# Merging the closing block of an attention and MLP kernel into the engines' main programs

## The reference

```
q = xn @ Wq (16 heads of 32); k, v = split(xn @ Wkv) (4 groups of 32)
scores = q k^T / sqrt(32), causal, + alibi slope * (s - t); attn = softmax(scores); o = attn @ v
attention = concat(o) @ Wo + bo
gate, up = xn @ Wg^T, xn @ Wu^T;  inter = gelu(gate) * up (4096 wide);  mlp = inter @ Wd^T
out = x + attention + mlp
```

## Time and profile before

| | |
|---|---|
| profiled execution | 1784.39 us, span 1782.6 |
| busy: PE, DVE, ACT, POOL | 95%, 75%, 60%, 53% of the span |
| PE's first matmul of the loop | at 120.18 |
| last matmul of the last slot | starts at 1688.39 |
| last sum of the MLP | DVE, starts at 1695.02, 0.69 us |
| granted clock, mean | 0.985 |

### The profile page before, as it was taken

The page is one execution under the profiler, slowest core; times in us unless marked ns, Lnnn a source line. Parts: engine busy times, 40 slices in busy tenths (PEclk is TensorE's granted clock), DMA queues, the critical chain, the costliest instruction groups (busy, mean ns, idle before and its releaser), DMA issues. The chain is left out here.

```text
span 1782.6 us, 31010 instructions
## 1 busy us (share of the span) xinstructions
PE 1693.1 (95%) x10368; PEld 848.4 (48%) x10368; DVE 1340.1 (75%) x2785; ACT 1075.6 (60%) x1779; POOL 953.2 (53%) x801
## 2 busy tenths in 40 slices
PE   4989999999999999999999999999999999999947
PEld 3754444444444444444444444444444444444435
DVE  6867777777777777777777777777777777777728
ACT  2436757575757676675757575766757575757610
POOL 3315647374646556473746465564737464645617
PEclk9989999999999999999999999999999999999968
DMA  6770120302020201203021202012030203020154
GB/s 190 208 195 16 29 59 17 75 24 74 26 72 20 75 17 44 56 16 80 20 73 26 74 20 74 16 47 52 20 80 17 73 26 74 23 70 17 48 176 149
DMA packets 94971, 110.04 MB, mean 62 GB/s; under 512 B 39085, under 2 KB 58541, under 8 KB 93021
## 3 DMA queue, kind: packets, MB, share of 16 engines
q1 hardware_dynamic: 94812, 108.05, 22.3%
HBM read 72.74 MB, written 22.41 MB: 53 GB/s over the span
## 5 line engine op out<-in xcount | busy, mean ns | idle before, releaser
L1409 POOL TENSOR_TENSOR plo<-p,phi 128x512 f16<-128x512 f32 (+1 forms) x576 | 659.0, 1151 | 327.8 <-ACT phi L1241 324.9
L1234 ACT ACTIVATE p<-score_ps,pshift 128x512 f32<-128x512 f32 (+1 forms) x576 | 382.1, 663 | 308.0 <-DVE score_ps L1321 154.4
L1241 ACT ACTIVATE phi<-p 128x512 f16<-128x512 f32 (+1 forms) x576 | 349.9, 607 | 15.3
L1417 POOL TENSOR_TENSOR il<-prod,ih 128x512 f16<-128x512 f32 x128 | 160.8, 1256 | 352.5 <-DVE ih L1315 352.5
L1141 PE MATMUL score_ps<-qst,kst 128*128 128x512 f32 (+3 forms) x640 | 308.0, 498 | 12.1 <-ACT p L1234 10.7
L1336 DVE TENSOR_REDUCE mxp<-max_ps 128x1 f32<-128x512 f32 x256 | 175.3, 685 | 53.9 <-PE max_ps L1119 53.9
L1283 DVE TENSOR_TENSOR acc<-down_ps,acc 128x512 f32<-128x512 f32 x253 | 172.7, 683 | 52.2 <-PE down_ps L1087 50.3
L1107 PE MATMUL gate_ps<-xh,wh 128*128 128x512 f16 x512 | 199.1, 389 | 0.0
L1107 PE MATMUL up_ps<-xh,wh 128*128 128x512 f16 x512 | 198.4, 387 | 0.0
L1087 PE MATMUL down_ps<-wh,ih 128*128 128x512 f16 x506 | 196.1, 387 | 0.9 <-DVE acc L1283 0.9
L1107 PE MATMUL gate_ps<-xh,wl 128*128 128x512 f16 x512 | 194.8, 380 | 0.0
(11 more groups left out here) (197 smaller groups left out, 2910.2 us busy)
## 6 DMA issues: line engine op xcount, KB each, us to landing
qst<-q_parts SPq DMA_DIRECT2D x204, 64.0 KB
kst<-k_parts SPq DMA_DIRECT2D x48, 256.0 KB, 4.7
o<-oraw SPq DMA_DIRECT2D x192, 64.0 KB
vst<-v_parts SPq DMA_DIRECT2D x17, 512.0 KB, 6.1
q_parts<-o SPq DMA_DIRECT2D x24, 256.0 KB, 3.4
raw<-L_ffn_gate_W_packed_dram SPq DMA_DIRECT2D x18, 256.0 KB, 2.8
raw<-n_L_ffn_up_W_packed_dram SPq DMA_DIRECT2D x18, 256.0 KB, 3.1
raw<-L_ffn_down_W_packed_dram SPq DMA_DIRECT2D x18, 256.0 KB, 3.9
```

The costliest lines, as they stand in the source:

```text
L1234: nc.scalar.activation(p32[n % PR][:, 0:cols], score_ps[:, 0:cols], ACT.Exp, bias=pshift[:, 0:1]).then_inc(exp_done, 1)
L1241: nc.scalar.activation(phi[n % PP][:, 0:cols], p32[n % PR][:, 0:cols], ACT.Copy).then_inc(phi_done, 1)
L1409: nc.gpsimd.tensor_tensor(plo[n % PP][:, 0:cols], p32[n % PR][:, 0:cols], phi[n % PP][:, 0:cols], ALU.subtract).then_inc(plo_done, 1)
L1417: nc.gpsimd.tensor_tensor(il[w % 2][:, a, :], prod[a][:], ih[w % 2][:, a, :], ALU.subtract).then_inc(il_done, 1)
```

## The change

The block `epilogue` is gone; what it did follows the loop in each engine's program, and parts of it stand in the last head.

- **Outputs as f16 pairs.** After `normalise` ACT rounds the head to f16 (`output_hi`, slot 38) and POOL takes the rest (`output_lo`, slot 39); `store_on` stores both, and the stored heads are loaded as operands without a conversion. `o_copy` no longer scales; the factor is applied at the very end (`yback`).
- **Wo as f16 pairs**, in the last head: SP loads it into the room of the decoded weights when the head starts; DVE finds its largest value (slots 26 to 29), a DRAM round trip spreads it (`spread_tops`), DVE makes the scale (slot 33), ACT and DVE the pair (slots 35 to 40). In that head nothing of a next head is loaded, decoded or turned.
- **Bias in the first sums.** The preamble stores the column scales and their inverses; the first sum into each tile of `acc` takes `bias * inverse` instead of cleared memory.
- **Row sums apart.** `gather_o` issues two transfers for them instead of four, ahead of the others, with a semaphore of their own.
- **Order after the loop.** PE projects two tiles before the MLP's last sums and six behind them, always the three full groups, in all eight banks; then the last group of these eight, and then the other eight tiles. ACT issues 18 transfers (x, stored heads) and then does the last `output_hi`; the results are made in `acc` and stored from it.

```diff
+    def output_hi(act, h):
+        act.wait_ge(on_done, h + 1)
+        if h:
+            act.wait_ge(on_out, 32 * h)
+        nc.scalar.activation(onh[:], on[:], ACT.Copy).then_inc(ohi_done, 1)
...
+    def output_lo(pool, h):
+        pool.wait_ge(ohi_done, h + 1)
+        if h:
+            pool.wait_ge(on_out, 32 * h)
+        nc.gpsimd.tensor_tensor(onl[:], on[:], onh[:], ALU.subtract).then_inc(olo_done, 1)
```

Preamble's SP, at its end, and the start of the loop:

```diff
                 store_v(NCH - 1)
+                sp.wait_ge(os_done, 1)
+                    sp.dma_start(os_s[0].rearrange("(k p) -> p k", p=P), oscale[:]).then_inc(os_out, 16)
+                    sp.dma_start(os_s[1].rearrange("(k p) -> p k", p=P), oinv).then_inc(os_out, 16)
...
+                sp.wait_ge(os_out, 32)
+                for row, src in ((column_inv, os_s[1]), (bias, bo)):
+                    sp.dma_start(row, src.rearrange("(o n) -> o n", o=1).broadcast_to([P, C])).then_inc(bias_in, 16)
...
-                nc.gpsimd.memset(acc[:], 0.0).then_inc(acc_done, 1)
+                pool.wait_ge(bias_in, 32)
+                nc.gpsimd.tensor_tensor(bias_row, bias, column_inv, ALU.mult).then_inc(acc_done, 1)
```

PE, ACT, DVE and SP after the loop:

```diff
+                pe.wait_ge(wo_lo, KVH)
+                pe.wait_ge(o_in[0], 16 * FULL_DMAS[0])
+                pe.wait_ge(red_done, after(HEADS * NMAX))
+                for n in range(2):
+                    project(n, first)
                 pe.wait_ge(gelu_done, after(HEADS * GU))
...
                 for t in range(TPC):
                     for half in range(2):
                         down(HEADS * NCH - 1, t, half, (down_ps, gate_ps, up_ps, score_ps)[t])
+                pe.wait_ge(oraw_done, after(2 * HEADS * NCH))
+                for n in range(2, TPC):
+                    project(n, first)
+                pe.wait_ge(o_in[1], 16 * FULL_DMAS[1])
+                for t in range(TPC):
+                    pe.wait_ge(acc_done, after((HEADS * NCH - 1) * TPC + t + 1))
+                    project(TPC + t, first)
+                for n in range(NT):
+                    if n % TPC == 0:
+                        pe.wait_ge(o_in[n // TPC], 16 * (FULL_DMAS[n // TPC] + 2))
+                        pe.wait_ge(last_in[n // TPC], 32)
+                    if n >= len(y_ps):
+                        pe.wait_ge(y_read, n - len(y_ps) + 1)
+                    project(n, last if n < len(y_ps) else range(KVH))
...
+                act.wait_ge(il_done, after(HEADS * GU))
+                load_x(act, 1)
+                act.wait_ge(on_out, 32 * LAST)
+                for c in range(2):
+                    load_rest(act, c)
+                act.wait_ge(up_done, HEADS * GU)
+                for c in range(2, NCH):
+                    load_x(act, c)
+                for c in range(2, NCH):
+                    load_full(act, c)
+                    load_rest(act, c)
+                output_hi(act, LAST)
+                act.wait_ge(ohi_done, HEADS)
+                load_last(act, 0, onh)
...
                 loop(dve, body)
+                scale_sums(0)
+                add_x(0)
                 for t in range(TPC):
                     accumulate((HEADS * NCH - 1) * TPC + t, (down_ps, gate_ps, up_ps, score_ps)[t])
+                scale_sums(1)
+                row_sums(dve, LAST)
+                add_x(1)
+                for c in range(2, NCH):
+                    scale_sums(c)
+                    add_x(c)
+                for n in range(NT):
+                    dve.wait_ge(y_done, n + 1)
+                    dve.wait_ge(base_done, n // TPC + 1)
+                    nc.vector.scalar_tensor_tensor(acc[:, n, :], y_ps[n % len(y_ps)][:], yback, acc[:, n, :],
+                                                   ALU.mult, ALU.add).then_inc(y_read, 1)
...
                 loop(sp, body)
+                load_sums(sp, LAST)
+                store_recips(sp, LAST)
+                spread_recips(sp, LAST)
+                sp.wait_ge(olo_done, HEADS)
+                load_last(sp, 1, onl)
+                for n in range(NT):
+                    sp.wait_ge(y_read, n + 1)
+                    sp.dma_start(out_d[n * P:(n + 1) * P, :], acc[:, n, :]).then_inc(out_done, 16)
```

`load_x` loads a quarter of x; `load_full` and `load_rest` load a quarter's columns of the stored heads, the three full groups and the rest of the fourth; `load_last` moves the last head, straight from its tile, to its place. `spread_recips` is now one transfer instead of four:

```diff
-        for c in range(NCH):
-            sp.dma_start(rb[c * HD:(c + 1) * HD, :], r_s[h % 2, c * CH:(c + 1) * CH].rearrange("(o t) -> o t", o=1)
-                         .broadcast_to([HD, CH])).then_inc(rb_in, 16)
+        sp.dma_start(rb[:], r_s[h % 2].rearrange("(c o t) -> c o t", o=1, t=CH).broadcast_to([NCH, HD, CH])
+                     ).then_inc(rb_in, 16)
```

More of the change, by code:

```diff
@@ L183, in build @@
         on_done = sem("on_done")
[L184 to L185 removed]
+        ohi_done = sem("ohi_done")
+        olo_done = sem("olo_done")
+        os_done = sem("os_done")
+        os_out = sem("os_out")
         with ExitStack() as work:
@@ new lines, in main_loop, with load_full @@
+        (load_sums, row_sums, store_recips, spread_recips, add_parts, normalise, output_hi, output_lo
+         ) = output_steps(nc, e, on, onh, onl, rb)
+        FULL = KVH - 1
+        FULL_DMAS = (2, 3, 2, 2)
+        def load_full(eng, c):
+            cols = slice(c * CH, (c + 1) * CH)
+            low = [(0, FULL, ocl_whole[c])] if c != 1 else [(0, 2, ocl_pair[0]), (2, FULL, ocl_pair[1])]
+            for part, g0, g1, dst in [(0, 0, FULL, och[c])] + [(1, *piece) for piece in low]:
+                eng.dma_start(dst[:, 0:g1 - g0, :], o_s[part, g0 * REP:g1 * REP, :, cols]
+                              .rearrange("(g r) d t -> (r d) g t", r=REP)).then_inc(o_in[c], 16)
@@ L967, in loop, with load_x @@
+        def load_x(eng, c):
+            tiles = TPC // len(xr[c])
+            for k, part in enumerate(xr[c]):
+                at = c * CH + k * tiles * P
+                eng.dma_start(part, x_d[at:at + tiles * P, :].rearrange("(j p) h -> p j h", p=P)).then_inc(x_back[c], 16)
         def loop(eng, body):
@@ L1196, in body, with project @@
                         mlp(s, 1)
-                        if s in TURN_W_AT:
+                        if s in TURN_W_AT and i < LAST:
                             m, a = TURN_W_AT[s]
                             turn_weights(pe, m, a, i + 1, (red_done, after((i + 1) * NMAX)))
-                loop(pe, body)
+                def project(n, groups):
+                    c, t = n // TPC, n % TPC
+                    for g in groups:
+                        for q, (part, rhs) in enumerate(((0, woh), (0, wol), (1, woh))):
+                            mm = nc.tensor.matmul(y_ps[n % len(y_ps)][:], out_part(part, c, g)[:, t * P:(t + 1) * P],
+                                                  rhs[:, g, :], start=(g == 0 and q == 0), stop=(g == KVH - 1 and q == 2))
+                    if KVH - 1 in groups:
+                        mm.then_inc(y_done, 1)
+                loop(pe, body)
+                first, last = range(KVH - 1), range(KVH - 1, KVH)
+                pe.wait_ge(wo_lo, KVH)
[3 more added lines that the diff above has]
+                    project(n, first)
                 pe.wait_ge(gelu_done, after(HEADS * GU))
@@ new lines, in wo_low, with scale_sums @@
+                def wo_low(g):
+                    dve.wait_ge(wscale_done, 1)
+                    dve.wait_ge(wo_hi, g + 1)
+                    nc.vector.scalar_tensor_tensor(wol[:, g, :], wo[g], wscale, woh[:, g, :], ALU.mult, ALU.subtract
+                                                   ).then_inc(wo_lo, 1)
+                def scale_sums(c):
+                    part = acc[:, c * TPC:(c + 1) * TPC, :]
+                    dve.wait_ge(acc_done, after((HEADS - 1) * NT + (c + 1) * TPC))
+                    if c == 0:
+                        dve.wait_ge(column_in, 16)
+                    nc.vector.tensor_tensor(part, part, column.unsqueeze(1).broadcast_to([P, TPC, C]), ALU.mult
+                                            ).then_inc(scaled, 1)
@@ L1390, in _, with add_x @@
+                def add_x(c):
+                    dve.wait_ge(scaled, c + 1)
+                    dve.wait_ge(x_back[c], 16 * len(xr[c]))
+                    tiles = TPC // len(xr[c])
+                    for k, x in enumerate(xr[c]):
+                        part = acc[:, c * TPC + k * tiles:c * TPC + (k + 1) * tiles, :]
+                        last = nc.vector.tensor_tensor(part, part, x, ALU.add)
+                    last.then_inc(base_done, 1)
                 dve.wait_ge(mask_done, 2)
                 loop(dve, body)
+                scale_sums(0)
@@ L1424, in body @@
                             normalise(pool, i - 1)
+                        if i and s == OUTPUT_LO_AT:
+                            output_lo(pool, i - 1)
                         if 1 <= s and PIECES[s - 1][0] == "up" and PIECES[s - 1][3]:
@@ L1595, in _round12 @@
+                for step in range(2):
+                    add_parts(pool, LAST, step)
+                normalise(pool, LAST)
+                output_lo(pool, LAST)
 def _round12(v):
```

397 lines of the change are left out of this document (184 added, 213 removed).

## The result

The changed kernel takes 1774.01 us (median of 4 runs, 1772.02 to 1774.97), the kernel before 1786.3 beside it: ratio 0.9929, 95% interval 0.9912 to 0.9947. It is 12 us faster, not 32: the direction was right, the size wrong, and 1774 lies outside the range. The profiled execution took 1774.28 us with a span of 1772.4, so the trace accounts for 1772.4 - 1782.6 = -10.2.

A forecast was written before the change was run, and what follows sets the result against it. TensorE, 95% busy, was taken as the bound up to the last head, then a 94.0 us serial tail. Tail and last head -40.4, start +1.1, heads +7.8 sum to -31.5 us: forecast 1753, range 1743 to 1763.

The forecast's parts named there:

- The start: Preamble's end: two more SP stores add +1.1 us of issuing; the bias wait counts nothing.
- two more now follow, and every engine waits for SP there: 2 x 0.53: Preamble's end: the two new column-scale stores cost 0.53 us of SP issuing each, +1.1 in all.
- The other thing that the paragraph feared: Loop's start: a late bias row would hold POOL's rests of the probabilities, a few us once; counted as nothing.
- Per head: Heads 1 to 14: output_hi at slot 38 adds 0.56 us each on ACT, unhidden, +7.8 in all.
- Last head: Last head in the loop: six turns of weights leave PE, 2.0 us saved; Wo's scale trip costs nothing.
- The tail: After PE leaves the loop: reordered sums and loads, PE waiting 3.8 us for the last head; predicted -38.4 us.
- 2.74: Tail: the store of the last head's reciprocals, in us.
- 0.4 + 1.97: Tail: spreading the last head's reciprocals before POOL's product, in us.
- a third more ... 1.2: Tail: 1.2 us added to the two small transfers because ACT's 5.3 MB of loads share the transfer engines.
- The loads hold the last head back: Rival, tail: ACT's 18 transfers and a slow row-sum load delay the last head, +8 us, 1761; chance 0.25.
- The slot hides the copy: Rival, heads: output_hi costs nothing at its slot, 1745 us; chance 0.16.
- ACT is held by POOL: Rival, heads: ACT waits behind POOL's product and stops exponentials; slower than before, 1801 at 4 us a head; chance 0.04.

The follow-up runs named there:

- e1: The changed kernel with the two column-scale stores in 128 pieces of 16 bytes instead of 512 of 4 (columns permuted): 1766.58 us, ratio 0.9890.
- e2: The changed kernel with one tiny one-column POOL operation behind the preamble's last PARTITION_ALL_REDUCE, stores unchanged: 1760.20 us, ratio 0.9857.
- e6: The kernel before the change with the same tiny POOL operation as e2: 1781.43 us against 1784.54, ratio 0.9982.
- e3: The changed kernel with output_hi in slot 40 instead of 38 and output_lo in 41 instead of 39: 1765.26 us, ratio 0.9885.
- e4: The changed kernel with Wo's scale made in slot 37 instead of 33 and its pair from slot 40 instead of 35: 1769.59 us, ratio 0.9909.
- e5: The changed kernel with ACT's loads of the last half of x (2 MB) behind the last head's pieces and their additions later: 1769.55 us, ratio 0.9915.
- e9: The changed kernel with the reciprocals spread in four transfers, as before the change, instead of one: 1776.24 us, ratio 0.9951.
- e7: The changed kernel with e2, e3, e4 and e5 together, and the last head's row sums ahead of scale_sums(1): 1747.39 us, ratio 0.9791.
- e10: e7 with e9's spreading, SP's third gather ahead of x, and ACT's last quarter of stored heads behind the last head's pieces: 1746.89 us, ratio 0.9783.

## Why the prediction was wrong, step by step

- **"The start", wrong, +11.8** (1.4 of it before the changed code). The step that failed is "two more now follow, and every engine waits for SP there: 2 x 0.53". The issue was priced and the landing was not, since nobody on the list waited for it. The row sat in the trace: `identr` with 7.7 of idle time released by "issue", at just this place. I read a gap without a releaser as fixed. e1 and e2 show that it is not: 17.6 beside the 4-byte stores, 9.8 beside 16-byte ones, 7.2 with none. Why POOL stands there at all is not shown by any run. The Trainium skill, "GPSIMD Engine Reference", section "2.1 Instruction dispatch", says that the first call of freshly loaded code pays about 6 us without an instruction in the profile. The trace agrees in kind (7.0 to 7.7 in before and after, at each change between elementwise operations and PARTITION_ALL_REDUCE at which POOL waited for nobody, but for the 17.6), though the gap comes at every such change and not at a first call alone. That such a load shares the transfer engines with the stores would explain the 17.6, and is argued only: in after the second store has landed at 132.9 and POOL goes on at 140.76, 7.8 later, as long as the whole gap of before, but no transfer of code stands in the trace there. The other thing that the paragraph feared cost nothing that shows: in e2 POOL waits 16.1 for the bias row, and from PE's first loop matmul to the first reciprocal it is 125.5, in e6, which has no such wait, 125.2.
- **"Per head", right**: +7.6 for +7.8, 0.81 at slot 40, and e3 takes it back by moving the copy.
- **"Last head", wrong, +4.7.** The step that failed is "all of it comes before slot 44, when the gather is due anyway: nothing": it was about SP's place and not about the trip's length, 11 us, which no term had. The sentence behind it, "if the scale came late, ACT's copies at slot 35 would hold PE, by some us", is what happened: 3.1, and behind it PE's matmuls are 0.43 apart instead of 0.22 (granted clock 0.73 from 1690 to 1696, by which I estimate 0.27 x 6 = 1.6 more). e4 takes both away; its last head is 68.3, as predicted (70.3 - 2.0).
- **"The tail", wrong by two terms, +5.0.** The mechanism and the order were right: row sums done 12.9 after PE's end of the loop (predicted 12.6), PE's wait ended by the last head's pieces, the slow matmuls behind it, 26 us without waits. The terms "2.74" and "0.4 + 1.97", with "a third more ... 1.2" for the shared engines, were 6.3 in all and measured 11.9; the rest of the sum came out 0.6 shorter. Two causes, each shown alone: contention with ACT's bulk (e5: 6.6 to 1.9), and the form of the spreading load, whose duration I had read off the last of four transfers (e9: 5.3 to 3.5). Late bulk can lengthen the spreading too (e4: 8.4). The Trainium skill, "DMA: Bandwidth & Descriptors", section "Rules for kernel authors", says that an outermost dimension of size c < 16 confines the whole transfer to at most c engines, with a leading broadcast of c copies as its example. This load has c = 4, and the trace agrees: share 0.25 of the 16 engines in one transfer, up to 0.46 in four, 5.3 against 3.5; I had not weighed it.
- **The rivals.** "The loads hold the last head back" came true in its cause, but at another transfer: ACT was done issuing by 1726.4, 10 us before POOL's product, and the row sums were in before DVE wanted them; the store of the reciprocals paid. The rule by which transfers of two engines share the same sixteen had been cited for it, and the runs bear it out (the store 6.6 at 326 GB/s, 1.9 at 45). "The slot hides the copy" and "ACT is held by POOL" are out.

The terms add up: +11.8 - 0.2 + 4.7 + 5.0 = 21.3, the gap between -31.5 and -10.2. Had the three been known, the forecast would have been 1774; e7 takes most of this away and gives 1747, below the 1753 forecast, because it also moves the copy that costs the 7.6 and takes away the gap of 7.7 that was there before (3 us, e6).

## What to carry to other kernels

Price a DMA by its pieces and by who shares the engines when it lands, not by the issuing time, also where nobody seems to wait for it: a gap without a releaser is not a constant and can grow with such traffic. Where a chain of small transfers sets the end, look for the bulk issued just ahead of it by any engine, and issue it behind. When a chain has been cleared, look at the engine beside it: nearly half of what e10 gained on the transfers went to POOL operations that DVE slowed.

## What the runs showed of the hardware

- 512 pieces of 4 bytes to memory took 9.5 and 11.4 us, 128 pieces of 16 bytes 1.9 and 2.8 (e1); a transfer of 128 pieces of 4 bytes 6.7, in the last head. Three loads of 256 KB issued behind the two stores landed after 12.2 to 12.8 us, behind those of 16-byte pieces after 4.1 to 5.7.
- A broadcast load with outermost dimension 4 kept the transfer engines' share at 0.25, at some 100 GB/s (e5); in four transfers it reached 0.46 (e10).
- POOL's change between PARTITION_ALL_REDUCE and elementwise arithmetic took 7.0 to 7.7 us, both ways, in before and after (17.6 beside the 4-byte stores); a MEMSET and a COPY passed without it (e2). An operation on a single column is enough to take it early.
- POOL's operations on two inputs of 128x512 took 2.42 and 3.18 where an operation of DVE on two inputs of 128x2048 in SBUF had started first (e9, e10), 1.15 and 1.26 alone. Where POOL's started first, it kept 1.26, and DVE's took 3.37 instead of 2.29 (e9).
